# A two-layer gated transformer block on one core: sums of the second weighing behind the fourth probabilities, the weighted norm in two places, a GpSimd sum later

## What is computed

```python
# x: (8, 256, 512); ctx: (8, 256, 512), used as keys and values of both attentions
x = x + tanh(g_xattn[0]) * causal_attention(layernorm(x), ctx, ctx)            # 16 heads of 32
x = x + tanh(g_ffn[0])   * ffn_ternary(layernorm(x), w_gate_up, w_proj)        # silu gate, rms norm
x = x + tanh(g_xattn[1]) * cross_attention(layernorm(x), ctx, q/k/v/o weights) # rms norm of q and k
x = x + tanh(g_ffn[1])   * bitlinear_ffn(layernorm(x), w_norm, w_gv, w_out)    # 8-bit activations, ternary weights
```

## Time and profile before

| what | value |
|---|---|
| device time, median of 3 runs | 1078.25 us (1078.14 to 1081.09) |
| the profiled execution | 1077.42 us, its span 1075.5 us |
| TensorE | 1042.7 us busy, 97% of the span |
| VectorE | 833.3 us busy, 77% |
| ScalarE | 586.3 us busy, 55% |
| GpSimd | 119.2 us busy, 11% |
| granted TensorE clock | 1.0 of full speed in all of the 40 slices |

### The profile page before, as it was taken

One profiled execution on the slowest core, in us unless ns is written; L12 is line 12 of the kernel. 1 busy time (PEld: TensorE's weight loads), 2 busy tenths in 40 slices (PEclk: granted clock), 3 DMA queues, 4 the chain that ended last, 5 costly groups with the idle time before them and its releaser, 6 DMA issues.

```text
span 1075.5 us, 24510 instructions
## 1 busy us (share of the span) xinstructions
PE 1042.7 (97%) x9813; PEld 623.3 (58%) x9898; DVE 833.3 (77%) x1440; ACT 586.3 (55%) x893; POOL 119.2 (11%) x212
## 2 busy tenths in 40 slices
PE   8899999999999999999999999999999999999998
PEld 3555555555777767777777655444444444444544
DVE  4988888778777665675666587888888888888987
ACT  4766667676433333333333356647575757573633
POOL 1101011010000000000000212230211111110110
PEclk9999999999999999999999999999999999999999
DMA  9475554542221120230211032314343434331223
GB/s 364 171 250 187 178 188 144 172 158 68 112 80 50 40 80 13 67 80 20 80 40 40 20 109 58 61 32 89 79 90 79 90 79 80 86 65 47 39 61 79
DMA packets 121200, 102.79 MB, mean 96 GB/s; under 512 B 94720, under 2 KB 95232, under 8 KB 120832
## 3 DMA queue, kind: packets, MB, share of 16 engines
q1 hardware_dynamic: 121088, 101.21, 33.7%
HBM read 65.54 MB, written 12.58 MB: 73 GB/s over the span
## 4 chain that ended last, share of the span: by engine, by line
PE 81%; DVE 10%; issue 4%; ACT 3%; DMA 2%; SPq 0%; POOL 0%; DVEq 0%; ACTq 0%; POOLq 0%
PE bank L704 10%; PE bank L705 10%; PE bank L792 10%; PE bank L669 9%; PE bank L810 9%; PE bank L919 5%; PE bank L937 4%; PE bank L907 4%; PE bank L888 3%; PE bank L869 2%; DVE ARENA L1800 2%; PE bank L549 2%; PE bank L601 2%; PE bank L574 2%; PE bank L622 2%
## 5 line engine op out<-in xcount | busy, mean ns | idle before, releaser
L704 PE MATMUL bank<-ARENA,W 128*128 128x256 f16 x1024 | 227.3, 273 | 0.7 <-issue 0.7
L705 PE MATMUL bank<-ARENA,W 128*128 128x256 f16 x1024 | 227.3, 273 | 0.0
L1107 ACT ACTIVATE ARENA<-ARENA 128x512 f16<-128x512 f32 (+1 forms) x96 | 66.9, 707 | 136.0 <-DVE ARENA L1755 132.7
L810 PE MATMUL bank<-ARENA 128*128 128x512 f32 x256 | 118.4, 603 | 2.2 <-DVE ARENA L1842 1.8
L919 PE MATMUL bank<-W,ARENA 128*128 128x512 bf16 x496 | 115.8, 379 | 3.9 <-DVE W L1916 1.9
L669 PE MATMUL bank<-ARENA 128*128 128x512 f32 x256 | 117.8, 602 | 1.0 <-DMA ARENA<-in_wkv 1.0
L792 PE MATMUL bank<-W,ARENA 128*128 128x512 bf16 x478 | 114.1, 379 | 2.0 <-issue 0.2
L704 PEld LDWEIGHTS bank<-ARENA,W 128*128 128x128 bf16 x1024 | 100.2, 98 | 19.1 <-issue 1.3
L705 PEld LDWEIGHTS bank<-ARENA,W 128*128 128x128 bf16 x1024 | 100.2, 98 | 18.0
L2219 POOL TENSOR_TENSOR ARENA<-ARENA 128x2 f32<-128x2 f32 (+1 forms) x72 | 51.4, 714 | 481.7 <-DVE ARENA L1529 248.1
L1755 DVE SCALAR_TENSOR_TENSOR ARENA<-bank,ARENA 128x512 f32<-128x512 f32 x64 | 48.0, 750 | 66.4 <-PE bank L705 63.0
(11 more groups left out here) (190 smaller groups left out, 1746.2 us busy)
## 6 DMA issues: line engine op xcount, KB each, us to landing
W<-in_w SPq DMA_DIRECT2D x48, 512.0 KB, 3.9
ARENA<-in_w SPq DMA_DIRECT2D x24, 512.0 KB, 3.3
kv_store<-ARENA SPq DMA_DIRECT2D x32, 256.0 KB, 4.1
W<-kv_store SPq DMA_DIRECT2D x15, 512.0 KB, 4.6
ARENA<-in_ctxT SPq DMA_DIRECT2D x8, 512.0 KB, 3.7
X<-in_x SPq DMA_DIRECT2D x8, 512.0 KB, 6.6
ARENA<-in_ctx SPq DMA_DIRECT2D x8, 512.0 KB, 6.1
out<-X SPq DMA_DIRECT2D x15, 256.0 KB, 2.7
```

The source lines that it names most:

```text
L704: pe.matmul(bank[:, i * S:(i + 1) * S], W0[:, at:at + P], xt_half(b, 0)[:, k, :], start=(k == 0), stop=False)
L705: mm = pe.matmul(bank[:, i * S:(i + 1) * S], W0[:, at:at + P], xt_half(b, 1)[:, k, :], start=False, stop=(k == KD - 1))
L810: mm = pe.matmul(to, src[:, k, t * P:(t + 1) * P], WQ[w][:, k, :], start=(k == 0), stop=(w == "o" and k == KD - 1))
L1107: return act.activation(to, src, ACT.Copy)
```

## The change

It reorders work and changes no arithmetic.

- Turns 3 to 7, TensorE: of the second weighing only the products with the values stay in place; the 8 matmuls for its sums move behind the fourth probabilities. Bank lists: w3 and y1 change places.
- Turns 3 to 7, VectorE: the second half of the weighted norm moves behind the row maxima; statistics and norm of the next batch's tokens and the store of the first out product move ahead of the second weighing's reading.
- Turn 2 of the third stage, GpSimd: `c_add_bias(2)` moves behind `c_rstd(3)`.
- Last turn of the attention, TensorE: a quarter of `b_gate_up(0, 1)` moves ahead of the last weighing.
- Turn 2 of the attention, VectorE: `a_max_rows(1, 0)` moves ahead of the statistics.

```diff
--- before.py
+++ after.py
@@ -267,7 +267,7 @@
         places.put(4, "xt0", 3)
         places.put(5, "xt1", 3)
         for turn in range(3, NB):
-            places.turn(turn, ("g0 v1 g3 pq0 v6 w0 y0", "v0 po1 v3 g4 v5 g7 w2", "po0 g2 v4 v7 pq1 w1 w3", "g1 v2 g5 g6 mt y1"))
+            places.turn(turn, ("g0 v1 g3 pq0 v6 w0 y0", "v0 po1 v3 g4 v5 g7 w2", "po0 g2 v4 v7 pq1 w1 y1", "g1 v2 g5 g6 mt w3"))
         places.turn(NB, ("g0 v1 g3 v5 v7 w1 w3", "v0 v3 g6 g7 y0", "po0 g2 g4 g5 mt w0", "g1 v2 v4 v6 po1 w2"))
         places.last.update({n: (s.c_ex, 8 * NB) for n in range(4)})
         a, b, c = NB - 3, NB - 2, NB - 1
@@ -894,19 +894,20 @@
                         if kb == 1:
                             mm.then_inc(s.c_st, 1)
 
-            def c_weigh(b, g):
+            def c_weigh(b, g, parts=(0, 1)):
                 to, sem, value = bank_c(f"w{g}", b)
                 pe.wait_ge(sem, value)
                 pe.wait_ge((s.ld_v0, s.ld_v1)[b % 2], 16 * (b // 2 + 1))
                 pe.wait_ge(s.c_ex, 8 * b + 2 * g + 2)
-                for what in range(2):
+                for what in parts:
                     for kb in range(TB):
                         for j in range(4):
                             h = 4 * g + j
                             lhs = keep["ones"] if what else bufW["V"][:, kb, h * DH:(h + 1) * DH]
                             mm = pe.matmul(part(to, j)[:, what * S:(what + 1) * S], lhs, bufC["PT"][:, h % 8, kb * S:(kb + 1) * S],
                                            start=(kb == 0), stop=True, skip_group_check=True)
-                mm.then_inc(s.c_pv, 1)
+                if parts[-1]:
+                    mm.then_inc(s.c_pv, 1)
 
             def d_value_gate(d, j):
                 t, n = j // 4, j % 4
@@ -956,10 +957,11 @@
                 for p in range(8):
                     if (b, p) == (0, 0):
                         b_gate_up(0, 0, (1,), (1,))
+                        b_gate_up(0, 1, (0,), (0,))
                         a_weigh(NB + 1, NB - 1, 1)
                         a_sum(NB + 1, NB - 1, 1)
                     elif (b, p) == (0, 1):
-                        b_gate_up(0, 1, (0,))
+                        b_gate_up(0, 1, (0,), (1,))
                         a_turn_sums(NB + 1, NB - 1)
                         b_gate_up(0, 1, (1,))
                         a_turn_out(NB + 1, NB - 1)
@@ -1056,9 +1058,10 @@
                 c_probs(b, 1)
                 c_weigh(b, 0)
                 c_probs(b, 2)
-                c_weigh(b, 1)
+                c_weigh(b, 1, (0,))
                 d_out_product(d, 0)
                 c_probs(b, 3)
+                c_weigh(b, 1, (1,))
                 c_weigh(b, 2)
                 c_weigh(b, 3)
                 d_out_product(d, 1)
@@ -1645,6 +1648,7 @@
                 f, b, e, last = turn, turn - 1, turn - 2, turn - 3
                 front, back, end = f < NB, b >= 0, e >= 0
                 late = turn in (1, NB)
+                rows_first = late or turn == 2
                 if back:
                     a_scores(b, 0)
                     if not front:
@@ -1660,7 +1664,7 @@
                     a_max_parts(b, 0)
                     if not front:
                         b_turn_first()
-                    if late:
+                    if rows_first:
                         a_max_rows(b, 0)
                     if turn == 1:
                         a_distance(b, 0)
@@ -1672,7 +1676,7 @@
                     v.tensor_copy(keep["identf"], pre["cst"][:, 0:P])
                     v.tensor_copy(keep["identb"], pre["cst"][:, 0:P])
                     v.tensor_copy(bufA["block"], pre["cst"][:, P:2 * P]).then_inc(s.const, 1)
-                if back and not late:
+                if back and not rows_first:
                     a_max_rows(b, 0)
                 if front:
                     v.wait_ge(s.a_xt, 2 * f)
@@ -1868,11 +1872,11 @@
                     bn = v.bn_aggr(keep["mvd"][:, t, :], keep["statsd"][:, t, :])
                 bn.then_inc(s.d_st, 1)
 
-            def d_weighted(d):
+            def d_weighted(d, ts=range(TB)):
                 v.wait_ge(s.d_st, d + 1)
                 v.wait_ge(s.d_q, 2 * d)
                 v.wait_ge(s.ld_wn, 16)
-                for t in range(TB):
+                for t in ts:
                     v.scalar_tensor_tensor(out=bufC["h"][:, t, :], in0=xt_of(d, t), scalar=keep["mvd"][:, t, 0:1], in1=bufC["wn"],
                                            op0=ALU.subtract, op1=ALU.mult).then_inc(s.d_hw, 1)
 
@@ -2117,7 +2121,7 @@
                 c_scores(b, 2)
                 d_largest(d, 3)
                 d_scale_u(d, 0)
-                d_weighted(c)
+                d_weighted(c, (0,))
                 d_value_gate(d, 4)
                 c_norm_q(f, 0)
                 c_scores(b, 3)
@@ -2125,6 +2129,7 @@
                 d_gated(d, 5)
                 d_gated(d, 6)
                 c_max_rows(b)
+                d_weighted(c, (1,))
                 d_integers16(d, 0)
                 d_gated(d, 7)
                 d_largest(d, 5)
@@ -2135,13 +2140,12 @@
                 c_norm_q(f, 1)
                 c_weigh(b, 0)
                 d_integers16(d, 1)
-                c_weigh(b, 1)
                 if f + 1 < NB:
                     stats(f + 1, s.c_ve)
-                c_weigh(b, 2)
-                if f + 1 < NB:
                     c_norm_x(f + 1)
                 d_store(d, 0)
+                c_weigh(b, 1)
+                c_weigh(b, 2)
                 c_weigh(b, 3)
                 d_store(d, 1)
 
@@ -2318,10 +2322,12 @@
                     c_queries_root(f, 1)
                 if c == 0:
                     d_line(c)
-                if c <= 0:
+                if c < 0:
                     c_add_bias(f)
                 if f + 1 < NB:
                     c_rstd(f + 1)
+                if c == 0:
+                    c_add_bias(f)
 
         with nc.Block() as block:
             block.sync(sync_program)
```

## The result

| | before | after |
|---|---|---|
| device time, median of 22 runs each | 1077.98 us (1077.01 to 1081.09) | 1079.97 us (1079.30 to 1082.38) |
| the profiled execution | 1077.42 us | 1079.95 us |
| its span | 1075.5 us | 1078.2 us |
| TensorE busy | 1042.7 us | 1042.8 us |

The ratio is 1.002, with a 95% interval of 1.0013 to 1.0026. By the medians the changed kernel is 2.0 us slower, by the interval of the ratio 1.4 to 2.8, which is within 0.3%.

The account below looks back on a forecast made before the run. The prediction took TensorE, 97% busy, as the bound. It summed -2.0 - 0.88 + 3.75 + 0.2 = +1.1 us, giving 1078.5 against the profiled execution and 1079.3 against the median of runs, range 1074.8 to 1082.0.

Parts of the forecast that it names:

- GpSimd sum: Third stage, before L810 at 701.87: moving GpSimd's additions frees two held VectorE instructions; gain 2.0 us, bounds 0 and 2.26.
- gate quarter: Last attention turn, stall at 280.21: eight gate matmuls fill TensorE's 0.89 us wait; gain 0.88, bounds 0 and 0.89.
- sums, turns 4 to 7, with the exponentials' stall: Out product waits for bank 4, sums are paid behind the fourth probabilities: 0.7 us a turn, 2.8, plus the stall's growth.
- sums, turn 3: In turn 3 the out product starts as now and the moved sums come on top: loss 0.95 us.
- the norm in two places: Turns 4 to 7: moving half the norm removes up to 0.28 of TensorE's 0.32 us stall at 838.88, worth nothing.
- rows in turn 2 of the attention: Statistics come some 1.3 us later, VectorE's 0.93 idle at 70.19 absorbs it: 0, upper bound 0.3 us.
- VectorE's delay: Turns 4 to 7: idle time from the moved half norm makes the first weighing's reading 0.33 to 0.55 us later.
- What the sums were to hide: Fourth exponentials wait for the moved sums; TensorE's 0.33 us stall at 859.57 stays, grows 0.05 five times: 0.2 loss.
- all after it 0.9 earlier: Sign of being right: no 0.89 us stall before the attention's last weighing, and everything behind it 0.9 us earlier.
- Rival 1: Bank 4 doesn't hold the out product and the sums cover the exponentials: -5.6 us, 1072.6; chance 0.13 with milder forms.
- Rival 2: No GpSimd gain: at the new place GpSimd holds something that ends on TensorE; +3.1 us, 1081.3; chance 0.10.
- Rival 3: VectorE about 1.0 us or more late at the first weighing, losing waits to ScalarE's gates; +3.9 us, 1082.1; chance 0.13.

Follow-up runs that it names:

- e4: The kernel before with only GpSimd's two additions moved later and the gate quarter moved ahead of the last weighing: 1074.33 us, ratio 0.9967.
- e1: The changed kernel with the second weighing whole again, its sums ahead of the first out product: 1076.62 us, ratio 0.9986.
- e10: The changed kernel with the second weighing's sums, the weighted norm and the attention's turn 2 rows as before: 1074.63 us, ratio 0.9975.
- e2: The changed kernel with the row maxima of the attention's turn 2 back behind the statistics: 1079.28 us, ratio 1.0013.
- e6: The kernel before with only the row maxima of the attention's turn 2 moved ahead of the statistics: 1079.05 us, ratio 1.0008.
- e3: The changed kernel with y0 and w3 exchanged in the bank lists, so the first out product uses bank 7: 1076.84 us, ratio 0.9993.
- e7: The changed kernel with the weighted norm whole at its old place: 1078.16 us, ratio 1.0002.
- e8: The changed kernel with y0 and w3 exchanged, the norm whole and turn 2's rows as before, sums still moved: 1074.91 us, ratio 0.9976.

## Why the prediction was right in its sum, and where it was wrong

It gave +1.1 us and 1079.3; measured were +2.0 by the medians, +2.8 by the intervals of the two traces, and 1079.97. In part the nearness is luck: the median before that it set out from, 1078.25 of three runs, is 0.27 above that of 22. By the traces, 1.7 us are missing in its sum, and they are two terms that it had at nothing. By its terms, from the intervals:

| term | predicted | measured | from |
|---|---|---|---|
| GpSimd sum | -2.0 | -1.99 | after; -1.97 in e4 |
| gate quarter | -0.88 | -0.87 | after; -0.86 in e4 |
| sums, turns 4 to 7, with the exponentials' stall | +2.8 and +0.16 | +2.85 | e1 against after |
| sums, turn 3 | +0.95 | +0.89, with the jitter of the transfers in it | e1 against after |
| the norm in two places, on TensorE, turns 4 to 7 | 0 | +0.53 | e10 against e1 |
| rows in turn 2 of the attention | 0, at most 0.3 | +1.21 | after, e2, e6 |

**The GpSimd sum** held to a hundredth: the two instructions fell to 0.16 and 0.17 us, and what TensorE got was VectorE's time, 2.0, not the 2.26 of its two stalls: L810 still starts 0.06 behind VectorE's last reading. The difference is the idle 0.16 at 698.44 and 0.12 ahead of L810. One piece of its evidence was weaker than it looked. It compared L1916 beside the additions with L1916 at 723.67, but the next pair of additions runs there too, from 723.44 to 725.95. L1916 at 840.87, beside no addition, takes 0.75 as well, so the conclusion stands. The rule of the Trainium skill (page "SBUF — State Buffer", section "Who interferes with whom") named only the norm as an instruction that could be held at the new place; the trace agrees in that it alone is longer there, but by 0.09 us, where the whole rest of the additions from its start, 708.01 - 707.67 = 0.34, would have been the hold. The spans of GpSimd are rough, so this one case doesn't decide the size of the hold.

**The gate quarter** held: the stall is filled to its end by eight matmuls that were to be done anyway.

**The second weighing's sums.** Their sum for turns 4 to 7, 2.96 with the exponentials' share, was right to 0.11 (2.85), but two of its steps were off by about 0.2 us a turn each, and they nearly cancel, which is luck. That the bank of the first out product holds it, and not TensorE's arrival, is shown by e3. What is paid behind the product came as reckoned: first to second out product 9.94 us in place of 8.98, 0.96 for the predicted 0.98. What comes back ahead of it follows from the start of the product, which the prediction put at the end of VectorE's reading + 0.1 ("some 0.1 us for the semaphore"). It is 0.28 or 0.29 after it, in all five turns; that the 0.16 which stood ahead of this product before is part of this is likely, but no run takes it apart. Before, the product started 852.68 - 851.90 = 0.78 after that end, so even with VectorE on time only 0.49 of the 0.93 can be used, not 0.68, and e7, where it is on time (796.94 before, 797.57 there, with an offset of 0.64 at the product ahead), shows that: four turns 1.81 us longer than in e10, 0.45 a turn and not the lower bound of 0.25.

The other step is VectorE's delay, predicted as 0.33 to 0.55. Taken from the second out product of the turn ahead, its reading came 0.22, 0.57, 0.48 and 0.24 later in turns 4 to 7 than before. In turn 4 that is 796.58 - 796.94 + 0.58, and in turn 5 it is 852.16 - 851.48 - 0.11. The product then starts 0.78 - 0.29 less that delay earlier: 0.27, -0.08, 0.01 and 0.25, and 0.27, -0.08, 0.02 and 0.26 were measured. So turns 4 and 7 lie in the predicted 0.13 to 0.35 and turns 5 and 6 don't. The sums themselves cost 0.71 or 0.72 in each turn all the same (after against e1), which is 0.96 - 0.49 and a delay of 0.24; what turns 5 and 6 have beyond that is the norm's, in the next paragraph. The turns became 55.23, 55.58, 55.48 and 55.23 us long, where the prediction wanted to see 55.1 to 55.3.

**The norm in two places** is what the prediction priced on VectorE alone, while TensorE was only to lose a stall ("it is worth nothing"). Here a step is missing: TensorE meets the moved half itself, in L810, whose bank waits for the last L1920. With the sums in place (e1 against e10) that costs 0.53 over four turns, all of it in turns 5 and 6 (54.87 and 54.77 us; turns 4 and 7 are 54.52 and 54.51). With the sums moved (after against e7) the split costs 1.57, and 0.52 when the out product has a bank of its own (e3 against e8). Seen from the other side, moving the sums costs 1.81 with the norm whole and 2.85 with the norm split. Once the sums are moved, the reading of the first weighing decides when the product starts, and the split delays that reading; with the sums in place (e1) the product has only its 0.16 ahead of it, so TensorE's own later arrival covers the delay.

That turns 4 and 7 don't pay can be read: with the norm split as with it whole (e1, e10) this L810 starts 34.87 us behind the second out product of the turn ahead, so the stall of 0.39 takes the place of the 0.31 before the last gate quarter. In turn 6 there was no stall at the gate quarter to lose, but one of 0.28 before L878, which ScalarE ends and which stays; L810 starts 35.13 behind. In turn 5 it starts 35.22 behind, with a stall of 0.75, and why that one is longer isn't settled. In turns 5 and 6 VectorE waits 0.45 and 0.36 us before the second L1920 of its pair, by the rows once for TensorE's product and once for ScalarE's gate, and less in turn 4, and no run tells why the two are late there.

**What the sums were to hide.** As predicted, the exponentials wait for the last of the moved sums, so the stall stayed; it grew by 0.09 where 0 to 0.1 was predicted (its five times 0.05 are 0.25, and not the 0.2 of the sum, which changes nothing). e8 shows it by itself: four turns 0.39 longer than e10's. The reordered end of the turn, put at nothing, held too: e10 keeps it and has four turns of 218.14.

**The rows in the attention** are the term that was mis-sized, and the largest miss: predicted 0 with an upper bound of 0.3, measured 1.21, outside its bound. Because of it the sign "all after it 0.9 earlier" didn't show either: behind the last weighing of the attention the changed kernel is 0.35 later, not earlier. The step said that the statistics come 1.3 us later and that VectorE has 0.93 idle at 70.19, "0.4 left". The 1.3 was right (1.35, 60.27 to 61.62). What it left out is what VectorE does between: the reciprocals at 63.85, whose bank TensorE takes at 64.42, about 5 us before VectorE's idle time that was to take the delay up. e4 confirms how narrow it was: in the old order, with TensorE there a little earlier, L669 already waits 0.32 us for these reciprocals. The cover must be looked for ahead of the first consumer, not anywhere behind. e6 shows the cost with that edit alone.

**The rivals.** Rival 1, that the product isn't held and the sums pay: its first half is refuted by the stall of 0.78 on L1846 and by e3, which takes it away, and its second by e8, where the product is free and nothing comes back. Rival 2, no gain from GpSimd: refuted by the interval from L549 to L810, 1.99 us shorter in the changed kernel and 1.99 or 2.00 in e1, e2, e3 and e7. Rival 3, VectorE 1.0 us later at the first weighing: it was 0.57 late at most, so its price didn't come. The forecast lay near because the terms with rows of their own were right; the two that were missing, 1.21 and 0.53, are small beside the range.

The best of the kernels is e4, with the GpSimd sum and the gate quarter alone, 3.6 us faster than before by its ratio; e10, with the harmless exchanges as well, can't be told from it.

## What to carry to other kernels

Work moved out of the way of a product helps only as far as the product's own bank is free; look first at who reads the bank last and when, since the end of that row, and the 0.3 us from there to the product's start, tell how much of the move can be used in a kernel like this one. When an instruction is delayed, walk through everything behind it on its engine up to the idle time that is to absorb it, and for each ask which bank or buffer it frees and how much slack the taker has; here 0.07 us of slack, 4 us behind the edit, was used up long before the idle time 9 us behind it. Two edits that delay one chain must be costed together: the norm's split cost 0.5 us by itself and 1.6 beside the moved sums.

## What the runs showed of the hardware

Two VectorE instructions of two elements a partition took 1.14 and 1.20 us beside GpSimd's additions of 128x512, and 0.16 and 0.17 without them. The same additions beside a norm of 128x512, a product read from a bank and a reduction cost 0.09 us in all. And the time from the end of VectorE's row to the start of the product that waited for it wasn't one number: 0.06 us at L810 behind turn 2, 0.15 at L810 in the middle of turn 5, 0.14 at L669, and 0.28 or 0.29 at the out product, which has 0.16 us ahead of it even when nothing holds it. The granted clock was 1.0 in every profiled execution.
